# Projection merged into the product for the logits, with the rows of rank, B and C sent to memory in the first stage

## What is computed

```python
xn = layernorm(x)
# selective state-space block
deltaBC = xn @ W_deltaBC.T                      # 64 rank + 16 B + 16 C columns
rank, B, C = split(deltaBC, [64, 80])
delta = softplus(rank @ W_dt.T + b_dt)          # 256 channels
hs[t] = exp(delta[t] * A) * hs[t-1] + delta[t] * B[t] * xn[t]   # 16 states per channel
y = sum over states of hs * C + D * xn
# experts, each picks 128 tokens of each batch
probs = softmax(xn @ Wg.T)                      # 8 experts
G, I = top_k(probs over the tokens, 128)
ffn = scatter_add(I, G * (gelu(xn[I] @ W1 + b1) @ W2 + b2))
out = x + y + ffn
```

## Time and profile before

| | |
|---|---|
| median of three runs | 2493.12 us (2491.65 to 2495.48) |
| profiled execution | 2495.35 us |
| its span, first to last instruction | 2493.5 us |
| busy: PE / DVE / ACT / POOL | 2356.9 / 2417.3 / 1971.3 / 2200.3 us |
| first stage, by its last x load | to about 114 us |
| picks after the first stage | 136.9 to 191.6 us |
| first and last scan | 193.2 and 2461.8 us |

### The profile page before, as it was taken

The page is one execution under the profiler, slowest core; times in us unless marked ns, Lnnn a source line. Parts: engine busy times, 40 slices in busy tenths (PEclk is TensorE's granted clock), DMA queues, the critical chain, the costliest instruction groups (busy, mean ns, idle before and its releaser), DMA issues. The chain is left out here.

```text
span 2493.5 us, 32910 instructions
## 1 busy us (share of the span) xinstructions
PE 2356.9 (95%) x10524; PEld 1773.7 (71%) x10524; DVE 2417.3 (97%) x2090; ACT 1971.3 (79%) x3432; POOL 2200.3 (88%) x1260
## 2 busy tenths in 40 slices
PE   7828999999999999999999999999999999999996
PEld 3306777777777777777777777777777777777775
DVE  6599999999999999999999999999999999999995
ACT  6627888888888888888888888888888888888783
POOL 4316999999999999999999999999999999999996
PEclk9958999999999999999999999999999999999998
DMA  9872455444445453454535344444444445453443
GB/s 303 274 270 69 136 167 140 117 124 112 135 117 137 102 137 108 117 132 98 154 99 146 95 133 107 127 123 117 133 116 125 108 115 133 100 150 93 106 91 53
DMA packets 162973, 325.38 MB, mean 130 GB/s; under 512 B 16272, under 2 KB 133104, under 8 KB 146160
## 3 DMA queue, kind: packets, MB, share of 16 engines
q1 hardware_dynamic: 95536, 239.11, 28.0%
q0 software_dynamic: 66048, 83.92, 20.1%
q10 hardware_dynamic: 1216, 0.23, 0.0%
HBM read 250.84 MB, written 84.93 MB: 135 GB/s over the span
## 5 line engine op out<-in xcount | busy, mean ns | idle before, releaser
L494 POOL TENSOR_TENSOR ysum<-ysum,prod 128x1024 f32<-128x1024 f32 x480 | 1307.1, 2723 | 33.4 <-DVE prod L905 24.4
L896 DVE TENSOR_TENSOR_SCAN bank_x<-decay,bank_x 128x1024 f32<-128x1024 f32 x512 | 1167.2, 2280 | 0.0
L1102 PE MATMUL bank_l<-ext,w_sb 128*128 128x256 f32 x4096 | 970.3, 382 | 0.8 <-ACT og L688 0.8
L1121 PE MATMUL bank_l<-w_sb,hid 128*128 128x256 f32 x4096 | 957.2, 383 | 0.0
L1121 PEld LDWEIGHTS bank_l<-w_sb,hid 128*128 128x128 f32 x4096 | 762.6, 190 | 163.4 <-issue 67.7
L1102 PEld LDWEIGHTS bank_l<-ext,w_sb 128*128 128x128 f32 x4096 | 756.5, 190 | 136.2 <-issue 23.5
L638 ACT ACTIVATE hid<-bank_l,b_all 128x256 f32<-128x256 f32 x1024 | 430.9, 475 | 332.6 <-PE bank_l L1102 329.4
L629 ACT ACTIVATE decay<-delta,a_sb 128x511 f32<-128x511 f32 x1024 | 640.0, 708 | 1.2
L905 DVE TENSOR_TENSOR prod<-bank_x,c_all 128x1024 f32<-128x1024 f32 x512 | 620.4, 1212 | 0.1
L842 DVE TENSOR_TENSOR bank_x<-du,bank_b 128x1024 f32<-128x1024 f32 x512 | 613.4, 1198 | 0.0
L513 POOL DMA_INDIRECT out<-og,idx_all x256 | 408.6, 1596 | 49.5 <-POOL ysum L494 35.4
(11 more groups left out here) (95 smaller groups left out, 1577.9 us busy)
## 6 DMA issues: line engine op xcount, KB each, us to landing
c_all<-c_rows SPq DMA_DIRECT2D x128, 1024.0 KB, 5.4
w_sb<-in_w SPq DMA_DIRECT2D x32, 1024.0 KB, 6.2
decay<-in_x SPq DMA_DIRECT2D x32, 512.0 KB, 5.4
xn_rows<-decay SPq DMA_DIRECT2D x32, 512.0 KB, 4.0
out<-yrow POOLq DMA_DIRECT2D x32, 512.0 KB
xr<-xn_rows SPq DMA_DIRECT2D x30, 512.0 KB, 6.5
ex<-xn_rows,idx_all POOLq DMA_INDIRECT x256
out<-og,idx_all POOLq DMA_INDIRECT x256, 4.1
```

The costliest lines, as they stand in the source:

```text
L494: nc.gpsimd.tensor_tensor(ysum[:, m % 2], first, prod[:, i], ALU.add).then_inc(sum_done, 1)
L896: nc.vector.tensor_tensor_scan(bank_x[:, s % 2], decay[:, k % 2, i].rearrange("p c t -> p (c t)"), bank_x[:, s % 2], 0.0, ALU.mult, ALU.ad ...
L1102: i = nc.tensor.matmul(bank_l[(q + k) % 2][:, (f % 2) * UT:(f % 2 + 1) * UT], w1_sb[:, e2, hc, f * P:(f + 1) * P], ext[:, k % 2, hc], star ...
L1121: i = nc.tensor.matmul(o, hid[:, (k - 1) % 2, f, c * K:(c + 1) * K], w2_sb[:, le2, f], start=False, stop=(f == FC - 1 and c == UB - 1))
```

## The change

The projection leaves the main loop. In the first stage the weights of the logits and of the projection stand side by side in `wpj_sb` (8 + 96 = 104 columns), and one product per batch gives 104 rows in a bank of its own (two banks in turn). ScalarE copies them to `proj` (four buffers). SP stores the 96 rows of rank, B and C to `bc_rows` in memory, and the 16 rows of B also into `b_whole`, where eight batches fill 128 partitions (`store_proj`, six rows behind the load). The logits are then turned batch by batch, 16 transposes per group instead of 4, and VectorE's copy and the wide weights go.

B is split into its three parts for eight batches at a time: group 0 where `take_bc` stood for batch 0, groups 1 to 3 after the first decays and ahead of the first gather. SP stores the parts to `b_rows` (`store_parts`), for groups 1 to 3 ahead of the residual copies 4 to 7. In the main loop SP loads 64 rows of rank into `rank` (`load_rank`) and 3 x 16 rows of B into `bcs` (`load_b`) for each batch; the C half of `bcs` stays zero. `load_c` reads `bc_rows`. The projection, the three copies, the two subtractions and the four moves of each batch go.

```diff
--- before.py
+++ after.py
...
+PJ = E + BC
+SPLIT = P // N
+NG = NB // SPLIT
...
-        c_rows = nc.dram_tensor("c_rows", [NB, N, T], F32, kind="Internal").ap()
+        bc_rows = nc.dram_tensor("bc_rows", [NB, BC, T], F32, kind="Internal").ap()
+        b_rows = nc.dram_tensor("b_rows", [3, NB * N, T], BF16, kind="Internal").ap()
...
-        wdbc_sb = sb("wdbc_sb", [P, HC, BC])
+        wpj_sb = sb("wpj_sb", [P, HC, PJ])
...
-        bc_all = sb("bc_all", [BC, T])
-        bc_hi = sb("bc_hi", [P, T], BF16)
-        bc_mid = sb("bc_mid", [P, T], BF16)
-        bc_lo = sb("bc_lo", [P, T], BF16)
-        bc_rest = sb("bc_rest", [P, T])
+        rank = sb("rank", [R, T])
+        b_parts = sb("b_parts", [P, 3, 2, T], BF16)
         bcs = sb("bcs", [3 * 2 * N, 2, T], BF16)
...
-        wg_wide = small(HC * GATE, GATE * E)
-        lgt = small(1, T)[0:GATE * E, 0]
...
+        proj = prod[0:PJ, 2:4, :, :].rearrange("p a b t -> p (a b) t")
+        b_whole = ysum[:, :, :, :].rearrange("p a b t -> p (a b) t")
...
+            def store_proj(b):
+                held(proj_done, b + 1)
+                sp.dma_start(bc_rows[b], proj[E:PJ, b % 4]).then_inc(proj_out[b % 4], 16)
+                sp.dma_start(b_whole[b % SPLIT * N:b % SPLIT * N + N, b // SPLIT],
+                             proj[E + R:E + R + N, b % 4]).then_inc(proj_out[b % 4], 16)
+            def store_parts(g):
+                for part, done in enumerate((hi_done, mid_done, lo_done)):
+                    held(done, g + 1)
+                    sp.dma_start(b_rows[part, g * P:(g + 1) * P, :], b_parts[:, part, g % 2]).then_inc(parts_out[g % 2], 16)
+            def load_b(nb, par, used):
+                g = (nb - 1) // SPLIT
+                held(parts_out[g % 2], (g // 2 + 1) * 48)
+                held(b_ready, used)
+                held(stack_set, 1)
+                for part in range(3):
+                    sp.dma_start(bcs[2 * N * part:2 * N * part + N, par],
+                                 b_rows[part, nb * N - N:nb * N, :]).then_inc(b_in[par], 16)
+            def load_rank(nb):
+                held(z_done, nb * 2 - 2)
+                sp.dma_start(rank[:], bc_rows[nb - 1, 0:R, :]).then_inc(rank_in, 16)
...
+                    if there(b - 6, NB):
+                        store_proj(b - 6)
...
+            for r in range(4):
+                held(proj_out[r], 32 * NB // 4)
+            load_rank(1)
+            store_parts(0)
+            load_b(1, 0, 0)
...
-            def move_high(nb, par, used):
-                held(all_done, nb)
-                sp.dma_start(c_rows[nb - 1], bc_all[BC - N:BC, :]).then_inc(c_out, 16)
-                held(hi_done, nb)
-                held(b_ready, used)
-                sp.dma_start(bcs[0:32, par], bc_hi[64:96, :]).then_inc(hi_moved, 16)
-            def move_mid(nb, par):
-                held(mid_done, nb)
-                sp.dma_start(bcs[32:64, par], bc_mid[64:96, :]).then_inc(mid_moved, 16)
-            def move_low(nb, par):
-                held(lo_done, nb)
-                sp.dma_start(bcs[64:96, par], bc_lo[64:96, :]).then_inc(lo_moved, 16)
             def load_c(u):
-                held(c_out, (u // SLOTS + 1) * 16)
                 held(prod_done, (u - 1) * STEPS)
                 first = u % SLOTS * STEPS
-                sp.dma_start(c_all[:, u % 2], c_rows[u // SLOTS:u // SLOTS + 1, first:first + STEPS, :]
+                sp.dma_start(c_all[:, u % 2], bc_rows[u // SLOTS:u // SLOTS + 1, R + N + first:R + N + first + STEPS, :]
                              .broadcast_to([P, STEPS, T])).then_inc(c_in[u % 2], 16)
-            move_high(1, 0, 0)
-            move_mid(1, 0)
-            move_low(1, 0)
             load_c(0)
+            for g in range(1, NG):
+                store_parts(g)
             for part in range(4, HALF // UB):
...
+                    if sl == 0 and there(b + 1, NB):
+                        load_rank(b + 2)
                     if sl == 1 and there(b + 1, NB):
-                        move_high(b + 2, (m + 1) % 2, b * N)
-                    if sl == 2 and there(b + 1, NB):
-                        move_mid(b + 2, (m + 1) % 2)
-                    if sl == 3 and there(b + 1, NB):
-                        move_low(b + 2, (m + 1) % 2)
...
-            def take_rest(nb):
-                pool.wait_ge(all_done, nb)
-                pool.wait_ge(hi_done, nb)
-                wait(pool, lo_done, nb - 1)
-                nc.gpsimd.tensor_tensor(bc_rest[0:BC, :], bc_all[:], bc_hi[0:BC, :], ALU.subtract).then_inc(rest_done, 1)
-            def take_lo(nb):
-                pool.wait_ge(mid_done, nb)
-                wait(pool, lo_moved, nb * 16 - 16)
-                nc.gpsimd.tensor_tensor(bc_lo[0:BC, :], bc_rest[0:BC, :], bc_mid[0:BC, :], ALU.subtract).then_inc(lo_done, 1)
+            def split_rest(g):
+                pool.wait_ge(hi_done, g + 1)
+                nc.gpsimd.tensor_tensor(b_whole[:, g], b_whole[:, g], b_parts[:, 0, g % 2], ALU.subtract).then_inc(rest_done, 1)
+            def split_lo(g):
+                pool.wait_ge(mid_done, g + 1)
+                wait(pool, parts_out[g % 2], g // 2 * 48)
+                nc.gpsimd.tensor_tensor(b_parts[:, 2, g % 2], b_whole[:, g], b_parts[:, 1, g % 2], ALU.subtract).then_inc(lo_done, 1)
...
-            take_rest(1)
-            take_lo(1)
+            split_rest(0)
+            split_lo(0)
             take_delta(1, 0)
             take_du(1, 0, 16)
+            for g in range(1, NG):
+                split_rest(g)
+                split_lo(g)
             pool.wait_ge(picks_done, 2)
             gather(0)
...
+                    if there(b - 3, NB):
+                        act.wait_ge(logits_done, b - 2)
+                        wait(act, proj_out[(r - 3) % 4], (b - 3) // 4 * 32)
+                        wait(act, lg_tr, (b - 3) // GATE)
+                        nc.scalar.copy(proj[:, (r - 3) % 4], lg_banks[(r - 3) % 2][0:PJ, :]).then_inc(proj_done, 1)
...
-            def take_bc(nb):
-                act.wait_ge(bc_proj, nb)
-                wait(act, rest_done, nb - 1)
-                wait(act, z_done, nb * 2 - 2)
-                wait(act, c_out, nb * 16 - 16)
-                nc.scalar.copy(bc_all[:], bank_t[0:BC, :]).then_inc(all_done, 1)
-                wait(act, hi_moved, nb * 16 - 16)
-                nc.scalar.copy(bc_hi[0:BC, :], bank_t[0:BC, :]).then_inc(hi_done, 1)
+            def split_hi(g):
+                for r in range(4):
+                    act.wait_ge(proj_out[r], (g + 1) * SPLIT // 4 * 32)
+                wait(act, parts_out[g % 2], g // 2 * 48)
+                nc.scalar.copy(b_parts[:, 0, g % 2], b_whole[:, g]).then_inc(hi_done, 1)
+            def split_mid(g):
+                act.wait_ge(rest_done, g + 1)
+                wait(act, parts_out[g % 2], g // 2 * 48)
+                nc.scalar.copy(b_parts[:, 1, g % 2], b_whole[:, g]).then_inc(mid_done, 1)
...
-            take_bc(1)
-            take_mid(1)
+            split_hi(0)
+            split_mid(0)
             for dt in range(HC):
                 take_z(1, 0, dt)
             softplus_exp(1)
             softplus_ln(1)
             act.wait_ge(zero_set, 1)
             decays(0, 0, 0, 0, 1, range(STEPS))
+            for g in range(1, NG):
+                split_hi(g)
+                split_mid(g)
...
+            nc.vector.memset(bcs[:], 0.0).then_inc(stack_set, 1)
...
-                    if r % GATE == 3 and there(g - 1, NB // GATE):
-                        dve.wait_ge(logits_done, g * GATE)
-                        wait(dve, lg_tr, g - 1)
-                        nc.vector.tensor_copy(lgt, lg_banks[gp][0:GATE * E, :]).then_inc(lgt_done, 1)
...
-                        pp, place = (r - 1) % 2, (r - 1) % GATE
-                        lg = lg_banks[(r - 1) // GATE % 2]
+                        pp = (r - 1) % 2
                         pe.wait_ge(xnt_done, b * 2)
-                        if place == 0:
-                            wait(pe, lgt_done, q * 2 + (r - 1) // GATE - 1)
+                        wait(pe, proj_done, b - 2)
                         if b == 1:
-                            pe.wait_ge(wide_set, 1 + HC * GATE)
+                            pe.wait_ge(params_in, 16 * 7)
                         for hc in range(HC):
-                            i = nc.tensor.matmul(lg[0:GATE * E, :], wg_wide[:, hc * GATE + place], xtr[:, pp, hc],
-                                                 start=(place == 0 and hc == 0), stop=(place == GATE - 1 and hc == HC - 1))
+                            i = nc.tensor.matmul(lg_banks[pp][0:PJ, :], wpj_sb[:, hc], xtr[:, pp, hc],
+                                                 start=(hc == 0), stop=(hc == HC - 1))
                         i.then_inc(logits_done, 1)
                     g = q * 2 + r // GATE
                     if r % GATE == 1 and there(g - 1, NB // GATE):
-                        pe.wait_ge(lgt_done, g)
+                        pe.wait_ge(proj_done, g * GATE)
```

(54 more changed lines are left out.)

28 lines of the change are left out of this document (5 added, 23 removed).

## The result

The changed kernel takes 2507.96 us (median of four runs, 2507.10 to 2509.28) beside 2493.05 for the kernel before: ratio 1.0055, 95% interval 1.0042 to 1.0068, so 14.9 us or 0.6% slower. The profiled execution has a span of 2507.5 us, 14.0 more than before. The end shifts with the start of the scan: here are the scan's row (min/median/max in ns, first and last start) and VectorE's waits (in total, times, longest), to be read beside the earlier trace rows.

What follows compares the result with a forecast made beforehand. VectorE was taken to bound the scan loop, and a three-batch loop of x loads to pace the first stage. Stores +8, TensorE and ScalarE +2, removed copies -6 gave +4 on the median 2493.12: 2497 us, range 2487 to 2511.

Steps and rivals of the forecast that it cites:

- Scan loop: Main loop: the removed work lies beside VectorE, which waits for none of it; 0, bounds 0 to +2 us.
- Transfers: First stage: 229 KB of added stores per batch, partly filling holes between loads; +8 us, bounds 6 to 15.
- A rule that speaks against it: First stage: the skill page's 138 GB/s for 64 KB transfers would make the sum 27 us higher.
- TensorE and ScalarE: First stage: more transposes and a copy per batch, mostly in the loop's shadow; +2 us, bounds 0 to 6.
- Removed: First stage: VectorE's eight logits copies and the waits before them go; -6 us, bounds -3 to -12.
- Between the first stage and the scan: Picks cover the new chain, and slack covers a gather delay of 0 to 5 us; cost 0, bound +3.
- Rival C: Early scan: later groups' splits hold the first gather and the second slot's decays; 2509 us, chance 0.04.
- The sum: Whole kernel: +8 + 2 - 6 = +4 us, bounds -6 to +18.
- A: First stage: transfers are the limit, so stores add their full time; 2508 us, at half rate 2519; chance 0.22.
- B: First stage: VectorE's stop at the logits disturbs the loop, over half of 21.5 us returns; 2485 us, chance 0.11.
- D: Whole kernel: the loop absorbs both, nothing changes; 2493 us, chance 0.08 together with a small gain.
- Signs: Expected in the new trace: load timing and spacing, VectorE's waits, a DMA rate nearer 385 GB/s, first scan at 195 to 199.

Runs made afterwards that it cites:

- before_stores: The kernel before with only the added transfers per batch (96 rows of 2 KB stored, 16 moved within SBUF), read by nobody: 2508.47 us, ratio 1.0057.
- before_tiny: The kernel before with the same two added transfers per batch, each row cut to its first 64 bytes: 2499.24 us, ratio 1.0022.
- load_first: The changed kernel with SP loading the next x before it stores anything, same bytes and number of transfers: 2496.28 us, 1.0012 of the kernel before.
- before_actcopy: The kernel before with only VectorE's copy of the logits moved to ScalarE: 2488.98 us, ratio 0.9981.
- resid_first: The changed kernel with SP's residual copies 4 to 7 ahead of the stores of B's parts of groups 1 to 3: 2506.27 us, 1.0050 of the kernel before.
- before_both: The kernel before with the logits' copy on ScalarE and the next x loaded before the store, without the change itself: 2482.20 us, ratio 0.9954.

## Why the prediction was right or wrong

The direction and the range (2487 to 2511) hold. The likeliest value, 2497, is 11 us short: +4 forecast, +14.9 measured. Point by point:

**Scan loop, 0**: right. 4.44 us per step before and after, no wait.

**Transfers, +8 with bounds 6 to 15: mis-sized, 15.0 measured** (before_stores). This is the step that failed most. I saw the loop and that the issues lie in it, and priced them by the trace's single issues, 0.6 to 0.8 us per round; measured it is 1.55 us more up to the load's issue (2.01 against 0.46 on the median), and 0.32 us more in it. And I let the bytes hide in the holes: they cost some 9.3 us (before_tiny against before_stores), and the load's landing went from 5.4 to 6.2 us. The upper bound was the right number for another reason: it assumed full engines with the holes kept, and load_first shows that the engines weren't full.

**A rule that speaks against it**: the price of the Trainium skill, page "DMA: Bandwidth & Descriptors", section "Bandwidth", gave, as an estimate, 27 us on top of +4. That is 25 x (1.7 - 0.6), set against the upper bound of 15; in place of my 8 it would be 34. It also stretched the page, whose 138 GB/s is for one transfer of 64 KB issued from GpSimd, while the store here has 192 KB and comes from SP. The first stage with the transfers at their full size lost 15.0, at 7 KB 5.7 (before_tiny). This case's runs don't bear that rate out for small transfers that queue beside large ones.

**TensorE and ScalarE, +2**: 1.8 measured, not told apart from 0, so the runs neither confirm nor refute it. Sixteen transposes took 1.15 us, less than the 1.7 that I took.

```profile
62.27 1.15 PE L955 MATMUL bank_t<-ident,prod 8*128 8x8 f32 x16
```

**Removed, -6 with bounds -3 to -12**: -4.5. Nearly right in size, but not in its place. I looked for it in the loop, and behind the last load only for 2.4 us. Of the 16.1 us of stops 7.1 lay behind the last load, 6.05 of them in one copy, and there most of the gain came (4.9 of 6.6 us in the profiles of before_actcopy and the kernel before). In the loop VectorE's wait reappeared as a wait for x.

**Between the first stage and the scan, 0 with a bound of +3: wrong by 4**, and here a mechanism was missed. I followed the gather to ScalarE's decays, had counted 5 us of slack, and overlooked what stands behind it in TensorE's own list: the transposes for VectorE's picks. I put the gather's delay at 0 to 5 us by the splits on GpSimd; the splits were in time (GpSimd waited 13.03 us for the picks), but the copies that the change pushes back, from 145 to 179 us, run beside the gather and its landing takes 13.1 instead of 4.4 us (which of the transfers beside it holds it, resid_first left open). Rival C named the gather, with a wait in the second slot as its place; there is none.

**The sum** by medians: +15.0 + 1.8 - 4.5 + 4.3 = +16.6 against 14.9 measured, within what the four medians leave open (each interval is 2 to 4 us wide on either side).

**Rivals.** A gave 2508 with full engines as the cause: the number is right, the cause isn't. B (the logits' stop is the disturbance) asked for over half of 21.5 us and got 4.5; the 11.3 of before_both hold the order too. D is out.

**Signs.** VectorE's wait for x above 26.8 (54.1) and none on a matmul in the stage: right. Loads 12 and 15 apart 10.3 to 11.2 us: 42.79 to 53.66, 10.87, right, but over all loads it is 12.4 per three. The last load at 110 to 114: 122.74, wrong. The first scan at 195 to 199: 206.84, wrong. The rate nearer to 385: 325, wrong, and that was the sign that the loop and not the plateau pays. ScalarE's wait for the logits' matmul, the sign for TensorE as the limit: 6 of 32 rows, 6.4 us, so no.

## What to carry to other kernels

When a stage is a loop of load, compute and reload, look at what the issuing engine does between the event that frees the buffer and the next load, and put the load first: here the order alone was worth 3.4 us in the kernel before and 11.7 in the changed one, with not a byte less. Taking work off engines that don't set the pace gained nothing here, and a transfer pushed to a later place in a queue must be checked against everything that is urgent at that later time. Behind a wait in a list, look at each later instruction of the same engine, not only at the one that the waited-for data feeds.

## What the runs showed of the hardware

An issue on SP isn't of fixed length: the x load's took 367 ns at least and 458 on the median in the kernel before, 776 with up to 1699 in the changed one, where four transfers followed each other and the load came last, and 499 with the same four and the load first (load_first). In before_both, where nothing but the load and one store are issued and the load comes first, it took 368. Rows of 64 bytes don't make the issue short: the move's took 741 ns on the median and 512 at the least (before_tiny), 912 and 513 with rows of 2 KB (before_stores). The two added transfers per batch cost 0.09 us each in this loop with rows of 64 bytes (5.7 us for 64 of them) and 0.23 at their full size (15.0 us). Two gathers of 128 rows of 1 KB on GpSimd's queue took 4.4 to 4.5 us from the first issue to their user in eight kernels with nothing issued on SP in the 25 us ahead of them, and 11.1 to 13.1 us in six with several MB issued on SP's queue just before or beside them.
